# A GNN layer and a mixture-of-experts block on one core: gate logits moved from TensorE to VectorE for 11 of 14 units

## The reference

```
n  = layernorm(x)
x1 = x + segment_sum(n[src] * edge_weight, dst) @ W.T + b
z  = layernorm(x1)
gates = softmax(z @ gW + gb)                 # 4 experts
top 2 of the gates, softmax over these two   # the mixing weights
out = x1 + shared_mlp(z) + sum over the two experts of weight * expert_mlp(z)
```

## Time and profile before

| what | us |
|---|---|
| median of three runs | 397.91 |
| the profiled execution, its own time | 398.72 |
| its span | 396.6 |
| PE busy | 367.7 (93%) |
| PE weight loads busy | 295.9 (75%) |
| DVE busy | 243.5 (61%) |
| ACT busy | 202.0 (51%) |
| POOL busy | 273.5 (69%) |

### The profile page before, as it was taken

One profiled execution on the slowest core, in us unless ns is written; L12 is line 12 of the kernel. 1 busy time (PEld: TensorE's weight loads), 2 busy tenths in 40 slices (PEclk: granted clock), 3 DMA queues, 4 the chain that ended last, 5 costly groups with the idle time before them and its releaser, 6 DMA issues.

```text
span 396.6 us, 8051 instructions
## 1 busy us (share of the span) xinstructions
PE 367.7 (93%) x2419; PEld 295.9 (75%) x2419; DVE 243.5 (61%) x1013; ACT 202.0 (51%) x551; POOL 273.5 (69%) x294
## 2 busy tenths in 40 slices
PE   4998579999999999999999999999999999899984
PEld 3786457868787888888796877787878877767772
DVE  6659998984799698514688455462175442446541
ACT  2554795494388788504999532322049231244331
POOL 7777777777777777777777777777777777772000
PEclk9998668999999999999999999999999999999999
DMA  6999745944444544543343434343433344332000
GB/s 183 379 380 279 210 111 131 341 106 105 105 108 118 129 118 100 133 106 108 104 130 102 132 107 134 105 129 105 132 103 107 115 125 134 105 108 80 15 13 25
DMA packets 53855, 53.15 MB, mean 134 GB/s; under 512 B 32522, under 2 KB 43636, under 8 KB 53684
## 3 DMA queue, kind: packets, MB, share of 16 engines
q0 software_dynamic: 13536, 36.98, 31.8%
q1 hardware_dynamic: 35220, 10.01, 10.9%
q10 hardware_dynamic: 5056, 5.64, 4.1%
HBM read 46.12 MB, written 6.48 MB: 133 GB/s over the span
## 4 chain that ended last, share of the span: by engine, by line
PE 82%; ACT 6%; DMA 5%; DVE 3%; issue 2%; SPq 1%; ACTq 0%; DVEq 0%
PE agg_ps L1222 19%; PE hid_ps L1264 17%; PE window_ps L1155 8%; PE tok_ps L1313 5%; DMA x_sb<-in_x 5%; PE build_ps L1209 5%; PE agg_ps L1191 5%; PE agg_ps L1209 4%; PE tok_ps L1311 3%; PE hid_ps L1277 3%; PE hid_ps L1273 3%; PE mid_ps L1244 3%; ACT low_1h L920 2%; PE hid_ps L1209 2%; PE mid_ps L1234 1%
## 5 line engine op out<-in xcount | busy, mean ns | idle before, releaser
L834 POOL DMA_INDIRECT rows<-normalised_rows,src_all x246 | 236.2, 960 | 75.5 <-issue 74.3
L1222 PE MATMUL agg_ps<-xn_all,dense 128*128 128x256 f32 x350 | 80.3, 381 | 0.8 <-ACT dense L970 0.8
L1222 PEld LDWEIGHTS agg_ps<-xn_all,dense 128*128 128x128 f32 x350 | 65.3, 190 | 11.0 <-ACT dense L970 1.7
L1264 PE MATMUL hid_ps<-xt,pack 128*128 128x256 f32 (+2 forms) x336 | 71.4, 358 | 0.0
L1264 PEld LDWEIGHTS hid_ps<-xt,pack 128*128 128x128 f32 x336 | 56.4, 190 | 9.1 <-issue 3.6
L920 ACT ACTIVATE low_1h<-iota,lo_f 128x128 f32<-128x128 f32 x182 | 57.6, 393 | 0.5 <-ACT xn_all L906 0.5
L1635 DVE TENSOR_SCALAR high_node<-iota,hi_f,own_w 128x125 f32<-128x125 f32 x182 | 49.4, 357 | 4.5 <-PE build_ps L1209 2.9
L1008 ACT ACTIVATE h<-hid_ps,pack 128x256 f32<-128x256 f32 (+2 forms) x84 | 32.8, 441 | 37.4 <-PE hid_ps L1264 37.2
L818 POOL DMA_INDIRECT rows<-in_x,src_first x36 | 34.9, 968 | 11.0 <-issue 10.4
L1155 PE MATMUL window_ps<-rows,select 128*32 128x256 f32 x564 | 37.3, 394 | 0.9 <-DVE select L1585 0.9
L1209 PE MATMUL build_ps<-high_node,low_1h 128*128 128x125 f32 x184 | 27.8, 299 | 4.6 <-ACT low_1h L924 3.6
(11 more groups left out here) (172 smaller groups left out, 523.2 us busy)
## 6 DMA issues: line engine op xcount, KB each, us to landing
rows<-normalised_rows,src_all POOLq DMA_INDIRECT x246, 2.8
x_sb<-in_x SPq DMA_DIRECT2D x6, 512.0 KB, 9.0
normalised_rows<-xn_all ACTq DMA_DIRECT2D x6, 512.0 KB
records<-in_rec SPq DMA_DIRECT2D x184, 1.5 KB
out<-y SPq DMA_DIRECT2D x10, 256.0 KB
dense<-in_x_cols ACTq DMA_DIRECT2D x4, 512.0 KB, 9.9
pack<-in_packed SPq DMA_DIRECT2D x1, 1544.5 KB, 9.9
x_sb<-in_x SPq DMA_DIRECT2D x3, 256.0 KB
```

What stands on the lines that cost most here:

```text
L834: pool.indirect_dma_start(rows[:, b % RING * BATCH + pos, :], None, table[:, :], bass.IndirectOffsetOnAxis(ap=src_all[:, c:c + 1], axis=0) ...
L1222: last = pe.matmul(dense_ps[0:r, t * D:(t + 1) * D], dense[:, h, t * P:t * P + r], xn_all[:, h, :], start=(h == 0 and t == 0), stop=(h == ...
L1264: last = pe.matmul(by_half(u.hid_ps[b % 2])[:, m % 2, 0:tok], w, u.xt[:, k, 0:tok], start=(k == 0), stop=(k == KD - 1))
```

## The change

The gate logits of the units D3, G8 and G9 (`LAST_UNITS`) stay on PE as they were. For the other 11 units DVE computes them: after `normalise`, the new `gates` does one `tensor_tensor_reduce` per tile and expert on `xn` and a row of gate weights that is broadcast to all partitions, and its sum with the bias goes straight to `logit`. The broadcast load grows from 260 to 1284 columns. The products go to a scratch `gate_x` of two buffers. `turn` no longer waits for the copy of the mixing weights of the unit before but for `xt`; the mixing weights are transposed into `tok_ps`, for which `turn_gates` waits for `y` of the unit before. The statistics of the first gathered rows take the place of a table that is no longer used, three semaphores of the ranking become one, and the planner gets other ranks, costs and conditions, so that the list of each engine is made anew.

```
+LAST_UNITS = [DENSE[-1], *GATHERED[-2:]]
...
-RANKS = {"open": 3, "near": 0.105, "behind": 0.46, "dve_behind": 0.83, "act_behind": 1.65, "hurry": -2.49,
-         "batch": 5.25, "rawturn": 14.77, "rawlin": -17.2, "merge": 7.43, "windows": 19.55, "built": 0.44,
...
+RANKS = {"open": 3, "near": 0.024, "behind": 1.75, "dve_behind": -0.37, "act_behind": 1.23, "hurry": 6.29,
+         "batch": -14.13, "rawturn": 21.54, "rawlin": -3.63, "merge": 8.39, "windows": 10.09,
...
-            ("dve", "norm", 0.33 * T, lambda: needs(of("std"), prior("turn", one))),
-            ("pe", "turn", 0.05 + 0.2 * T, lambda: needs(of("norm"), prior("turned", one))),
+            ("dve", "norm", 0.33 * T, lambda: needs(of("std"), prior("turn", one), 0.0 if one in LAST_UNITS else prior("gates", one))),
+            ("pe", "turn", 0.05 + 0.2 * T, lambda: needs(of("norm"), prior("xt", one), prior("route", one) if one in LAST_UNITS else 0.0)),
...
-            ("pe", "gated", 0.24 * T, lambda: needs(of("xt"))),
+        ] + ([
+            ("pe", "gated", 0.41 * T, lambda: needs(of("xt"))),
+        ] if late else []) + [
...
+        ] + ([] if late else [
+            ("dve", "gates", 1.63 * T, lambda: needs(of("norm"))),
+        ]) + [
...
-            ("pe", "tgt", 0.05 + 0.05 * T, lambda: needs(of("mix"))),
+            ("pe", "tgt", 0.05 + 0.05 * T, lambda: needs(of("mix"), prior("finish", one), at("rawout", RAW_BATCHES - 1))),
...
+        row_stats = dst_i[:, 0:6 * ROW_SLOTS].bitcast(F32).rearrange("p (j s) -> p j s", s=6)
...
+        shared = sb("shared", [P, D + E * D + E])
+        gate_w_sb = shared[:, D:D + E * D].rearrange("p (e d) -> p e d", e=E)
+        gate_x = sb("gate_x", [P, 2, D])
...
+        tok_b = u.tok_ps[:, :].bitcast(BF16)
...
+                sp.dma_start(shared[:, :], every.to_broadcast([P, D + E * D + E])).then_inc(s_linear, 16)
...
             def turn(q):
                 pe.wait_ge(s["xn"], q + 1)
                 if q:
-                    pe.wait_ge(s["mixt"], q)
+                    pe.wait_ge(s["xt"], q)
+                if q and UNITS[q - 1] in LAST_UNITS:
+                    pe.wait_ge(s["top"], tops_before(q - 1) + 1)
...
-            def turn_gates(q):
+            def turn_gates(q, in_order=True):
                 pe.wait_ge(s["parts"], SPLIT * (q + 1))
-                if q == 0:
+                if q:
+                    pe.wait_ge(s["y"], q)
+                else:
                     pe.wait_ge(s_filled, 4)
+                if q == 0 and in_order:
+                    pe.wait_ge(s_raw_out, RAW_BATCHES)
                 for t in range(UNITS[q].T):
-                    last = pe.transpose(mid_b[0:MIXED, 2 * MT + t * P:2 * MT + (t + 1) * P],
+                    last = pe.transpose(tok_b[0:MIXED, t * P:(t + 1) * P],
...
+            def gates(q):
+                done = E * gated_tiles(q)
+                dve.wait_ge(s["xn"], q + 1)
+                for t in range(UNITS[q].T):
+                    for e in range(E):
+                        if done >= 2:
+                            dve.wait_ge(s_gate_x, done - 1)
+                        dve.tensor_tensor_reduce(
+                            out=gate_x[:, done % 2, :], in0=u.xn[:, t, :], in1=gate_w_sb[:, e, :], scale=1.0,
+                            scalar=gate_b_sb[:, e:e + 1], op0=ALU.mult, op1=ALU.add,
+                            accum_out=u.logit[:, t, e:e + 1]).then_inc(s_gate_x, 1)
+                        done += 1
...
             def route(q):
...
+                if UNITS[q] in LAST_UNITS:
+                    dve.wait_ge(s["gated"], n - gates_before(n))
+                    dve.tensor_tensor(u.logit[R], logit_ps[R], gate_b_sb.unsqueeze(1).to_broadcast([P, T, E]),
+                                      ALU.add).then_inc(s["top"], 1)
+                    dve.wait_ge(s["top"], tops_before(q) + 1)
+                else:
+                    dve.wait_ge(s_gate_x, E * gated_tiles(n))
```

More of the change, by code:

```diff
@@ L169 @@
 UNIT_ORDER = "G0 D0 G1 G2 D1 G3 G4 G5 D2 G6 G7 G8 D3 G9"
-RANKS = {"open": 3, "near": 0.105, "behind": 0.46, "dve_behind": 0.83, "act_behind": 1.65, "hurry": -2.49,
-         "batch": 5.25, "rawturn": 14.77, "rawlin": -17.2, "merge": 7.43, "windows": 19.55, "built": 0.44,
-         "rowstd": 15.95, "rawxt": -2.24, "rawout": 12.98, "low": 22.59, "select": 3.55,
-         "select_late": -1.3, "place": -20.25, "records": 11.53, "onehot": -3.9, "rowstats": 5.81,
-         "rowshifts": -8.25}
-BUILD_RANKS = (2.58, 16.22, -1.26, -10.69)
-MULT_RANKS = (-5.54, -8.91, 10.79, 17.88)
+RANKS = {"open": 3, "near": 0.024, "behind": 1.75, "dve_behind": -0.37, "act_behind": 1.23, "hurry": 6.29,
+         "batch": -14.13, "rawturn": 21.54, "rawlin": -3.63, "merge": 8.39, "windows": 10.09,
+         "built": 4.36, "rowstd": 12.04, "rawxt": 0.68, "rawout": 1.62, "low": 13.02, "select": -9.36,
+         "select_late": 9.36, "place": -28.93, "records": 5.14, "onehot": -0.31, "rowstats": 5.85,
+         "rowshifts": -3.11}
+BUILD_RANKS = (2.81, 5.7, -0.7, -12.23)
+MULT_RANKS = (-3.56, -9.3, 15.33, 19.62)
 GATHER_US = 1.256
@@ L230, in unit_steps @@
         q, T, half = units.index(u), u.T, max(0.42, u.tok / PAIR)
+        late = u in LAST_UNITS
         one = units[q - 1] if q else None
@@ L371, in offers @@
         for rank, u in enumerate(open_units):
+            passed = set()
             for step in left[u]:
                 if step[0] == engine:
+                    strand = step[1] in ("tgt", "spr")
+                    if strand in passed:
+                        continue
                     ready = step[3]()
@@ L377, in offers @@
                                     (step[1], u), step[2]))
-                    if engine == "pe" or step[1] not in ("h1a", "h1b", "h1", "ex", "gex"):
+                    if engine == "pe":
+                        passed.add(strand)
+                    elif step[1] not in ("h1a", "h1b", "h1", "ex", "gex"):
                         break
@@ L514, in build @@
         b3_sb = piece(8)
-        gate_w_sb = piece(9).rearrange("p (k e) -> p k e", k=KD)
-        shared = sb("shared", [P, D + E])
+        gate_wt_sb = piece(9).rearrange("p (k e) -> p k e", k=KD)
+        shared = sb("shared", [P, D + E * D + E])
         gnn_b_sb = shared[:, 0:D]
-        gate_b_sb = shared[:, D:D + E]
+        gate_w_sb = shared[:, D:D + E * D].rearrange("p (e d) -> p e d", e=E)
+        gate_b_sb = shared[:, D + E * D:D + E * D + E]
         b3_rest = sb("b3_rest", [P, D])
@@ L652, in build @@
         s_off = sem("s_off")
+        s_gate_x = sem("s_gate_x")
         s_keys = sem("s_keys")
@@ L664, in build @@
             "x1 stats var std rstd xn turned xt gated top low ex total inv gate gtop "
-            "ahead tied tied_before glow gex order rank kept ktotal kinv parts mix_turned mixt "
+            "ahead tied glow gex rank kept ktotal kinv parts mix_turned mixt "
             "h1a h1b h1 l2 h2 spread mixed end y").split()
@@ L696, in stores_before, with gates_before, tops_before, gated_tiles @@
             return sum(stores_of(unit) for unit in UNITS[:n])
+        def gates_before(n):
+            return sum(unit not in LAST_UNITS for unit in UNITS[:n])
+        def tops_before(n):
+            return 2 * n - gates_before(n)
+        def gated_tiles(n):
+            return sum(unit.T for unit in UNITS[:n] if unit not in LAST_UNITS)
         def gathered_before(n):
@@ L744, in load_weights @@
             def load_weights():
-                sp.dma_start(shared[:, :], every.to_broadcast([P, D + E])).then_inc(s_linear, 16)
+                sp.dma_start(shared[:, :], every.to_broadcast([P, D + E * D + E])).then_inc(s_linear, 16)
                 sp.dma_start(pack[:, :], packed).then_inc(s_w, 16)
@@ L1243, in gate_products @@
                     for k in range(KD):
-                        last = pe.matmul(logit_ps[:, t, :], u.xt[:, k, t * P:(t + 1) * P], gate_w_sb[:, k, :],
+                        last = pe.matmul(logit_ps[:, t, :], u.xt[:, k, t * P:(t + 1) * P], gate_wt_sb[:, k, :],
                                          start=(k == 0), stop=(k == KD - 1))
@@ L1848, in _ @@
                         normalise(q)
+                    elif name == "gates":
+                        gates(q)
                     elif name == "route":
@@ L1881, in _ @@
                     normalise(q)
+                    if UNITS[q] not in LAST_UNITS:
+                        gates(q)
                     route(q)
@@ L1920 @@
         np.asarray(L0_ffn_gW).reshape(KD, P, E).transpose(1, 0, 2))], axis=1)
-    every = np.concatenate([row(L0_gnn_b), row(L0_ffn_gb)], axis=1)
+    every = np.concatenate([row(L0_gnn_b), row(np.asarray(L0_ffn_gW).T), row(L0_ffn_gb)], axis=1)
     laid = [x, np.asarray(x).T, *chunks(src), *chunks(dst), *chunks(nxt), *chunks(edge_weight), rec,
```

33 lines of the change are left out of this document (13 added, 20 removed).

## The result

The changed kernel takes 395.37 us (median of 20 runs, 394.26 to 397.22), the kernel before, run beside it, 397.47 us (20 runs, 394.23 to 401.29). The ratio is 0.9952, 95% interval [0.9933, 0.9972]: a gain of 1.9 us (1.1 to 2.7), where 5.2 us were forecast. The profiled execution after took 394.67 us, with a span of 392.6 us; the one before had 398.72 and 396.6.

What follows compares the result with a forecast made beforehand. PE was taken to bound the kernel, with GpSimd's gathers 6 us behind. Last batch at 366.0 plus 25.4 gave a span of 391.4 us, 5.2 less, so 392.7 us from the median of 397.9; range 389.0 to 398.5.

Steps and rivals of the forecast that it cites:

- Part 1: Gates of 21 tiles off PE: 8.5 us removed (upper bound 10.4), all in the chain.
- PE's account: The span as PE's work sets it: 396.6 - 8.5 + 2.5 = 390.6 us.
- Part 2: Gates on VectorE: 84 operations of 0.417 us, 35.0 us; 2.5 us of new PE stall from 100 to 160 us.
- third rival: On VectorE an accumulating gate operation takes 686 ns, stalling PE 9.8 to 18.6 us; median 403.6 us; chance 0.09.
- second rival: VectorE becomes the bound from 100 to 220 us, stall 6.6 us; median 396.0 us; chance 0.30.
- Part 3: VectorE's gates on two SBUF tensors slow GpSimd's gathers: the last gather 2.5 us later (0 to 5.6).
- second bound: GpSimd's last gathered rows, 6 us behind PE: the final unit G9 can begin at most 6.0 us earlier.
- Parts 4 and 5: Turned weights in the spread's bank, cost 0; larger broadcast load, 0 at the end with 2.5 us as bound.
- Part 6: The new instruction list: no gain where PE is full; decides between 2.5 and 11.0 us of stall where VectorE is tight.
- The sum: Whole kernel: last batch at 366.0 plus 25.4 us to the end, span 391.4 us, 5.2 us less.
- With D3 ahead these 1.7 us go: 25.4: Last batch to end: G9's two waits for D3's work vanish, so 27.1 us become 25.4.
- The later of the two accounts decides: The span is the later of PE's 390.6 us and GpSimd's 391.4 us.

Runs made afterwards that it cites:

- after_thin_gathers: The changed kernel with one row gather in twelve left out of each of the 21 table batches; 395.87 us, ratio 0.9925 to the kernel before.
- before_less_pe: The kernel before with 60 of 350 records of dense products left out; 393.78 us, ratio 0.9904 to the kernel before.
- after_less_pe: The changed kernel with part of the dense products of D1, D2 and D3 left out; 396.02 us, ratio 0.9970 to the kernel before.
- old_ranks_to_120: The changed kernel, its list made with the old ranks up to 120 us of the plan and the new ones behind; 395.30 us, ratio 0.9970.
- before_fewer_gathers: The kernel before without the 6 row gathers of the last batch; 397.06 us, ratio 0.9992 to the kernel before.
- before_thin_gathers: The kernel before with one row gather in twelve left out of each of the 21 table batches; 397.50 us, ratio 0.9994.

## Why the prediction was wrong, and where it was right

**Part 1.** The work was right: 8.5 us less, the group down to 16 records. So, nearly, was what it does to PE's account: 369.5 - 8.5 + 2.5 puts PE at its last batch at 363.5 us, and where it had no rows to wait for (`after_thin_gathers`) it got there at 364.03. But "Before 340 us PE is full, so all 8.5 us were in the chain" is too strong as a rule. In `before_less_pe` 13.0 us less of the same engine's work brought its last batch forward by 4.3 us (365.22), and the waits, the later rows and the lower clock took the rest.

**Part 2.** A gate operation starts every 0.405 us (the timeline has them at 306.45, 306.86, 307.27), against 0.417 forecast; VectorE's sum is 272.3 against 276.7. The page "Vector Engine (DVE) Microarchitecture Reference" of the Trainium skill, section "Points that are easy to get wrong", gives half throughput to a scalar_tensor_tensor with two non-bf16 SBUF sources. The trace has another operation, a multiply-and-sum on two SBUF tensors with the accumulator read back in 78 ns beside the next one, and shows no halving for it; the third rival fell. From 100 to 160 us VectorE was not full but less busy than before (49.27 us for 51.16, where 62.2 were forecast): the new list puts only 16 of the 84 operations there, not 28. PE lost 0.3 us more than before in that stage, not 2.5; the lack showed later. The second rival was nearer to the truth than its 0.30 says: a quarter more gates cost 4.1 us, so VectorE had no room left.

**Part 3.** The last gather ended at 363.31 us, 2.6 later than before, for 2.5 forecast, and the mean was 972 ns for 970. That is luck in good part. The first table gather already starts 0.3 us later; of the 2.8 us that the gathers take longer, 1.1 lie in those beside gate operations alone and 1.6 in gathers beside other operations of VectorE; two waits for PE are gone. And last gathers of variants without any gate on VectorE ended at 360.94, 361.22, 362.40 and 365.40 us. As to the mechanism, the Trainium skill ("SBUF — State Buffer", section "Who interferes with whom") infers that a VectorE operation with two SBUF inputs spares descriptor generation; 8 long ones of 19 against 0 of 14 speak against that, as far as the delay is one of descriptor generation. The gather also reads its indices from SBUF (`src_all`), and no run here tells the two apart.

A reading was wrong by 0.9 us as well. The 2.8 us from issue to landing were added to the end of the last gather; they count from its start. In the change it starts at 362.37 and PE begins at 365.20, 2.83 later; in `after_less_pe` it is 362.66 and 365.55. So rows landed at 362.6 in the kernel before, not 363.5, and the second bound stood 6.9 us behind PE.

**Parts 4 and 5.** No wait of PE for the bank and none of VectorE for the loads appears; its first bias addition starts at 71.63 us (71.00 in the earlier trace rows). 0 was right as far as the trace tells, but the stall could not be tested: the new list issues the broadcast at 59.79 us instead of 64.63, and the 642 KB land in 5.1 us. **Part 6** held in one direction: no order that I tried was faster, while the old ranks cost 4.5 us.

**The sum.** The step that failed is the stretch from the last batch to the end: "With D3 ahead these 1.7 us go: 25.4". It took 27.4 us (392.6 - 365.20). Of it, up to the end of PE's last record, 22.65 us of the kernel before less the 1.7, 20.95 in all, were forecast and 23.4 measured. The last records of the change, of the kernel before, and of `old_ranks_to_120`:

```profile
388.35 0.27 PE L1345 MATMUL tok_ps<-b_parts,mix_t 79*53 79x256 bf16 x1
...
391.85 0.27 PE L1314 MATMUL tok_ps<-b_parts,mix_t 79*53 79x256 bf16 x1
...
387.60 0.27 PE L1356 MATMUL tok_ps<-b_parts,mix_t 79*53 79x256 bf16 x1
```

D3 was not ahead. The new list spreads D3's products up to 364.06 us, and D3's turn, gates and layers 1 to 3 lie behind the last batch among G9's; its layer 3 at 380.65 us holds up G9's layer 2 until 382.17. And where D3's turn and gates did stand ahead (`old_ranks_to_120`, last batch at 365.11), PE still took 22.8 us to its last record, for it waited 0.65 us for VectorE's `parts` and 1.42 for `h` instead. So the 1.7 us were not to be had by D3's place alone. What follows PE's last record, VectorE's last sum and the last store, took 4.0 us in the change, 4.5 in the kernel before and 5.5 there. The last batch at 365.2 (366.0 forecast) and 27.4 give the 392.6 of the trace.

"The later of the two accounts decides" is not refuted by these runs. The two accounts for the last batch, 363.5 and 366.0, were measured as 364.0 and 365.2 (each in one trace), so near each other that neither 12 to 13 us less of PE's work nor 21 gathers fewer brought anything clear of the noise, while both together brought 5.4 us; a plain maximum does that too. What it leaves out is that the accounts move each other, as `before_less_pe` shows.

**The rest is the execution that was profiled.** Between the two profiled executions lie 4.05 us (398.72 - 394.67), between the medians 2.10: the first was 1.25 us over the median of its 20 runs, the second 0.70 under. So of the 3.1 us by which the gain was overrated, 1.2 lie in the sum of the span (391.4 against 392.6: the stretch 2.0 too short, the last batch 0.8 too late) and 1.9 in the pair of executions. The range held. GpSimd has taken the largest share of the chain, as forecast, but it does not bound the kernel by itself.

## What to carry to other kernels

When a change takes work off the bounding engine and leaves the next bound within a few us, don't count on the whole distance to that bound. The second account can move too, and the first can lose clock where it begins to wait: 13.0 us less work brought 3.8 us here where 6 or more stood open. Test this slope by leaving work of that engine out of the kernel as it is, and count in the trace what the edit took out. Forecast what lies behind the last batch from the new order, not from the old one with a wait taken off. For the engine that receives the work, count how full it is by stage (here 37.8 of 40 us, at 69% of the span). And a forecast of less than 1% needs the profiled execution's place among its runs before its span is used.

## What was unexpected of the hardware

Leaving out all waits for rows did not make the runs steadier but wider (391.6 to 400.5 us), and the longest of them have the lowest mean granted clocks (0.959 and 0.962, against 0.989 in the shortest); the change had 394.3 to 397.2 us at 0.974 to 0.990. The kernel before spreads as widely at one and the same mean clock: of its runs at 0.987 in one session one took 395.1 us and another 398.6. One piece of that spread can be seen. In `before`, `before_fewer_gathers`, `before_less_pe` and `before_thin_gathers` PE takes the same 22.65 us from its last batch to its last record, but what follows up to the end of the span takes 4.5, 5.6, 5.6 and 5.5 us. Another is the gathers: in traces without gates on VectorE the end of the last one differs by up to 4.7 us (360.69 to 365.40). What sets either stays open, and with it why the changed kernel's spread is less than half as wide.
